# Cross attention in a three-stage decoder kernel: scores on 64 rows, probabilities split before they are turned

## The reference

```python
q = (xn @ Wq).reshape(b, n, 16, 64).transpose(0, 2, 1, 3)
kv = cn @ Wkv                      # k and v, 16 heads of 64 each
sim = jnp.einsum('bhid,bhjd->bhij', q * scale, k)
sim = jnp.where(context_mask[:, None, None, :], sim, neg)
attn = jax.nn.softmax(sim, axis=-1)
out = jnp.einsum('bhij,bhjd->bhid', attn, v)
return out.transpose(0, 2, 1, 3).reshape(b, n, INNER) @ Wo
```

## Time and profile before

| | us |
|---|---|
| median of 3 runs (lowest to highest) | 2422.98 (2419.88 to 2423.97) |
| the profiled execution | 2422.5 |
| its span, first to last instruction | 2420.4 |
| PE busy in the span | 2254.3 |
| DVE busy | 1734.5 |
| ACT busy | 1625.8 |
| POOL busy | 742.4 |
| mean granted TensorE clock | 0.962 |

### The profile page before, as it was taken

One profiled execution on the slowest core, in us unless ns is written; L12 is line 12 of the kernel. 1 busy time (PEld: TensorE's weight loads), 2 busy tenths in 40 slices (PEclk: granted clock), 3 DMA queues, 4 the chain that ended last, 5 costly groups with the idle time before them and its releaser, 6 DMA issues. The chain is left out here.

```text
span 2420.4 us, 61603 instructions
## 1 busy us (share of the span) xinstructions
PE 2254.3 (93%) x20194; PEld 1699.5 (70%) x20194; DVE 1734.5 (72%) x4722; ACT 1625.8 (67%) x3584; POOL 742.4 (31%) x1304
## 2 busy tenths in 40 slices
PE   5999999999994899999999999999999999779998
PEld 4776776786783567677767677777777777668886
DVE  4545544554643689888988898889888988466657
ACT  5546445545632688888888888888888888445444
POOL 1211211211213244444444444444444444100003
PEclk8999999999997799999999999999999999759999
DMA  5000000000002000000000000000000000203302
GB/s 140 29 1 1 0 0 0 0 0 0 0 1 74 25 15 10 14 8 14 9 13 11 12 14 8 14 8 14 8 14 8 14 1 1 71 2 105 105 1 61
DMA packets 45652, 50.08 MB, mean 21 GB/s; under 512 B 19120, under 2 KB 37664, under 8 KB 45504
## 3 DMA queue, kind: packets, MB, share of 16 engines
q1 hardware_dynamic: 45504, 48.45, 6.8%
HBM read 44.78 MB, written 3.67 MB: 20 GB/s over the span
## 5 line engine op out<-in xcount | busy, mean ns | idle before, releaser
L1398 POOL TENSOR_SCALAR p_norm<-p,p_rec 112x375 f32<-112x375 f32 x512 | 303.8, 593 | 699.7 <-DVE p_rec L1240 692.4
L1122 ACT ACTIVATE p<-s_neg,neg_max 112x375 f32<-112x375 f32 x512 | 310.6, 607 | 139.9 <-DVE neg_max L1235 107.7
L1244 DVE TENSOR_TENSOR pt_lo<-b_t,pt_hi 125x336 f16<-125x336 f32 x512 | 259.1, 506 | 96.4 <-ACT pt_hi L1128 82.4
L1013 PE MATMUL b_t<-ident,p_norm 112*125 112x112 f32 x1536 | 281.8, 293 | 15.0 <-POOL p_norm L1398 14.7
L1220 DVE SCALAR_TENSOR_TENSOR k<-b_pb,k 64x375 f16<-64x375 f32 x512 | 280.9, 549 | 13.5 <-ACT k L1113 3.2
L1235 DVE CUSTOM_DVE_ANT_0 s_neg<-b_s,mask_bias 112x375 f32<-112x375 f32 x512 | 275.7, 539 | 0.8 <-PE b_s L1007 0.7
L1113 ACT ACTIVATE k<-b_pb 64x375 f16<-64x375 f32 x512 | 243.0, 475 | 24.4 <-PE b_pb L64 21.4
L1013 PEld LDWEIGHTS b_t<-ident,p_norm 112*125 112x125 f32 x1536 | 211.2, 189 | 62.1 <-POOL p_norm L1398 39.9
L1128 ACT ACTIVATE pt_hi<-b_t 125x336 f16<-125x336 f32 x512 | 225.5, 440 | 12.0 <-PE b_t L1013 6.5
L646 POOL TENSOR_SCALAR_AFFINE_SELECT sm<-sm 112x448 f32<-112x448 f32 x128 | 71.4, 581 | 433.3 <-ACT sm L430 433.3
L1006 PE MATMUL b_s<-k,q_hi 128*112 128x375 f16 x512 | 170.1, 332 | 19.3 <-DVE neg_max L1235 18.0
(11 more groups left out here) (245 smaller groups left out, 6593.7 us busy)
## 6 DMA issues: line engine op xcount, KB each, us to landing
w_raw<-in_L_ffn_W_dram SPq DMA_DIRECT2D x16, 1024.0 KB, 7.5
ctx<-in_ctx_dram SPq DMA_DIRECT2D x32, 375.0 KB
out_dram<-c_z SPq DMA_DIRECT2D x8, 448.0 KB, 3.2
x_sb<-in_x_dram SPq DMA_DIRECT2D x1, 3136.0 KB, 19.1
ff<-in_L_attn_w_dram SPq DMA_DIRECT2D x2, 1024.0 KB, 7.3
b_stage<-in_L_xattn_Wkv_dram SPq DMA_DIRECT2D x2, 1024.0 KB, 10.5
mask<-in_mask_BxS_bf_dram SPq DMA_DIRECT2D x32, 41.0 KB, 2.6
a_raw<-in_L_attn_wq_dram SPq DMA_DIRECT2D x1, 1024.0 KB, 5.0
```

What stands on the lines that cost most here:

```text
L1013: mm = pe.transpose(t_ps[h % 2][0:JP, t * T:(t + 1) * T], p_norm[:, h % 4, t * JP:(t + 1) * JP], ident[0:T, 0:T])
L1122: act.activation(p32[:, h % 4, :], s_neg[:, h % 2, :], ACT.Exp, bias=neg_max[:, h % 4:h % 4 + 1], scale=-1.0, accum_out=p_sum[:, h % 4:h % ...
L1244: dve.tensor_tensor(pt_lo[:, h % 4, :], t_ps[h % 2][0:JP, 0:JT * T], pt_hi[:, h % 4, :], ALU.subtract).then_inc(pt_lo_done, 1)
L1398: pool.tensor_scalar(p_norm[:, h % 4, :], p32[:, h % 4, :], p_rec[:, h % 4:h % 4 + 1], 0.0, ALU.mult, ALU.add).then_inc(p_norm_done, 1)
```

## The change

Five things are done at once, all in `layer2`.

1. Keys and queries are stored as high and low tiles for pairs of heads (`k2_hi`, `k2_lo`, `q2_hi`, `q2_lo`: `KI` = 8 pairs, a head in each 64-row half). ScalarE and VectorE write a key piece with one instruction of 128 rows each instead of two of 64, a query piece with one instead of four and two. The zeros of `qz_lo` go.
2. `scores` computes two heads at once, on even steps only: three products, each as two matmuls of 64 rows, the even head on the upper and the odd one on the lower rows, into the two banks `s_ps`. It waits until all earlier heads are masked, where it waited for all but one.
3. The normalised probabilities are written as fp16 (`p_hi`, GpSimd), and VectorE computes the low half `p_lo` from `p32`, the reciprocal and `p_hi` before they are turned. TensorE turns both with six fp16 transposes against an fp16 identity, into one bank seen as 1024 fp16 columns. ScalarE takes all 672 columns out with one copy (`take_turned`); the subtraction behind the turning goes.
4. VectorE's order in a step becomes: low half of the piece, `p_low` of head s + 1, reciprocal of head s + 2, `mask_max` of head s + 4.
5. TensorE's 32 batches are all written out; the other engines keep their loops.

```diff
-k2 = sb("k2", [P, 2, H, SP2], F16)
+k2_hi, k2_lo = (sb(f"k2_{n}", [P, 2, KI, SP2], F16) for n in ("hi", "lo"))
-q2_hi = sb("q2_hi", [P, 2, H, T], F16)
-qz_lo = sb("qz_lo", [P, 2, H, T], F16)
+q2_hi, q2_lo = (sb(f"q2_{n}", [P, 2, KI, T], F16) for n in ("hi", "lo"))
-p_norm = sb("p_norm", [T, 4, S2], F32)
-pt_hi, pt_lo = (sb(f"pt_{n}", [JP, 4, JT * T], F16) for n in ("hi", "lo"))
+p_hi, p_lo = (sb(f"p_{n}", [T, 4, SP2], F16) for n in ("hi", "lo"))
+pt = sb("pt", [JP, 4, 2, JT * T], F16)
+ident16 = sb("ident16", [P, P], F16)
-t_ps = [psum(f"b_t{i}", [P, 512]) for i in range(2)]
+t_ps = [psum(f"b_t{i}", [P, 1024], F16) for i in range(2)]
...
 def scores(b, par, h):
     written(b, ("q", h // 8), ("k", h // 2))
-    at_least(pe, s_masked, H * b + h - 1)
-    ps, keys = s_ps[h % 2][0:T, 0:S2], k2[:, par, h, 0:S2]
-    pe.matmul(ps, q2_hi[:, par, h, :], keys, start=True, stop=False)
-    pe.matmul(ps, qz_lo[:, par, h, :], keys, start=False, stop=True).then_inc(s_ready, 1)
+    at_least(pe, s_masked, H * b + h)
+    for n, (q2, k2) in enumerate(((q2_hi, k2_hi), (q2_lo, k2_hi), (q2_hi, k2_lo))):
+        for r in range(2):
+            rows = slice(DH * r, DH * (r + 1))
+            mm = pe.matmul(s_ps[r][0:T, 0:S2], q2[rows, par, h // 2, :], k2[rows, par, h // 2, 0:S2],
+                           start=(n == 0), stop=(n == 2))
+            if n == 2:
+                mm.then_inc(s_ready, 1)
 def turn_scores(b, h):
-    pe.wait_ge(p_norm_done, H * b + h + 1)
-    at_least(pe, pt_lo_done, H * b + h - 1)
-    for t in range(JT):
-        mm = pe.transpose(t_ps[h % 2][0:JP, t * T:(t + 1) * T], p_norm[:, h % 4, t * JP:(t + 1) * JP], ident[0:T, 0:T])
+    pe.wait_ge(p_lo_done, H * b + h + 1)
+    at_least(pe, pt_done, H * b + h - 1)
+    for n, part in enumerate((p_hi, p_lo)):
+        for t in range(JT):
+            c = (n * JT + t) * T
+            mm = pe.transpose(t_ps[h % 2][0:JP, c:c + T], part[:, h % 4, t * JP:(t + 1) * JP], ident16[0:T, 0:T])
     mm.then_inc(t_ready, 1)
+    pe.wait_ge(pt_done, H * b + h + 2)
...
-        for n, (v2, pt) in enumerate(((v2_hi, pt_hi), (v2_hi, pt_lo), (v2_lo, pt_hi))):
+        for n, (v2, part) in enumerate(((v2_hi, 0), (v2_hi, 1), (v2_lo, 0))):
...
-                               pt[:, (h + r) % 4, keys], start=(t == 0 and n == 0), stop=last)
+                               pt[:, (h + r) % 4, part, keys], start=(t == 0 and n == 0), stop=last)
...
         if not is_last(b):
             piece(b + 1, 1 - par, s)
-        if s + AHEAD < H:
+        if s % 2 == 0 and s + AHEAD < H:
             scores(b, par, s + AHEAD)
-        elif not is_last(b):
+        elif s % 2 == 0 and not is_last(b):
             scores(b + 1, 1 - par, s + AHEAD - H)
...
+pe.wait_ge(ident16_done, 1)
...
-for h in range(AHEAD):
+for h in range(0, AHEAD, 2):
     scores(0, 0, h)
-batches(pe, body)
+for b in range(B):
+    body(b, b % 2)
...
     if kind == "q":
-        for r in range(2):
-            for rows in half_rows:
-                ins = act.activation(q2_hi[rows, par, 8 * j + r:8 * j + 8:2, :],
-                                     ps[half_rows[r], 0:4 * T].rearrange("p (m t) -> p m t", t=T), ACT.Identity,
-                                     scale=UNSCALE * DH ** -0.5)
+        ins = act.activation(q2_hi[:, par, 4 * j:4 * j + 4, :], ps[:, 0:4 * T].rearrange("p (m t) -> p m t", t=T),
+                             ACT.Identity, scale=UNSCALE * DH ** -0.5)
     elif kind == "k":
-        for r, rows in enumerate(half_rows):
-            ins = act.activation(k2[rows, par, 2 * j + r, 0:S2], ps[rows, 0:S2], ACT.Identity, scale=UNSCALE)
+        ins = act.activation(k2_hi[:, par, j, 0:S2], ps[:, 0:S2], ACT.Identity, scale=UNSCALE)
...
+    at_least(act, p_lo_done, H * b + h - 3)
...
-def turned_high(b, h):
+def take_turned(b, h):
     act.wait_ge(t_ready, H * b + h + 1)
     at_least(act, av_done, H * b + h - 3)
-    act.activation(pt_hi[:, h % 4, :], t_ps[h % 2][0:JP, 0:JT * T], ACT.Identity).then_inc(pt_hi_done, 1)
+    act.activation(pt[:, h % 4, :, :], t_ps[h % 2][0:JP, 0:2 * JT * T].rearrange("p (n c) -> p n c", n=2),
+                   ACT.Identity).then_inc(pt_done, 1)
...
     if kind == "q":
-        for r, rows in enumerate(half_rows):
-            heads = slice(8 * j + r, 8 * j + 8, 2)
-            ins = dve.scalar_tensor_tensor(qz_lo[rows, par, heads, :], ps[rows, 0:4 * T].rearrange("p (m t) -> p m t", t=T),
-                                           UNSCALE * DH ** -0.5, q2_hi[rows, par, heads, :], ALU.mult, ALU.subtract)
+        ins = dve.scalar_tensor_tensor(q2_lo[:, par, 4 * j:4 * j + 4, :], ps[:, 0:4 * T].rearrange("p (m t) -> p m t", t=T),
+                                       UNSCALE * DH ** -0.5, q2_hi[:, par, 4 * j:4 * j + 4, :], ALU.mult, ALU.subtract)
     elif kind == "k":
-        for r, rows in enumerate(half_rows):
-            h = 2 * j + r
-            ins = dve.scalar_tensor_tensor(k2[half_rows[1 - r], par, h, 0:S2], ps[rows, 0:S2], UNSCALE,
-                                           k2[rows, par, h, 0:S2], ALU.mult, ALU.subtract)
+        ins = dve.scalar_tensor_tensor(k2_lo[:, par, j, 0:S2], ps[:, 0:S2], UNSCALE, k2_hi[:, par, j, 0:S2],
+                                       ALU.mult, ALU.subtract)
...
-def turned_low(b, h):
-    dve.wait_ge(pt_hi_done, H * b + h + 1)
-    dve.tensor_tensor(pt_lo[:, h % 4, :], t_ps[h % 2][0:JP, 0:JT * T], pt_hi[:, h % 4, :],
-                      ALU.subtract).then_inc(pt_lo_done, 1)
+def p_low(b, h):
+    dve.wait_ge(p_hi_done, H * b + h + 1)
+    dve.scalar_tensor_tensor(p_lo[:, h % 4, 0:S2], p32[:, h % 4, :], p_rec[:, h % 4:h % 4 + 1], p_hi[:, h % 4, 0:S2],
+                             ALU.mult, ALU.subtract).then_inc(p_lo_done, 1)
...
-        turned_low(b, s)
-        if s + 3 < H:
-            mask_max(b, par, s + 3)
+        if s + 1 < H:
+            p_low(b, s + 1)
         elif not is_last(b):
-            mask_max(b + 1, 1 - par, s + 3 - H)
+            p_low(b + 1, 0)
         if s + 2 < H:
             sum_reciprocal(b, s + 2)
         elif not is_last(b):
             sum_reciprocal(b + 1, s + 2 - H)
+        if s + AHEAD < H:
+            mask_max(b, par, s + AHEAD)
+        elif not is_last(b):
+            mask_max(b + 1, 1 - par, s + AHEAD - H)
...
-dve.wait_ge(zeroed, 1)
 for s in range(NCH):
     piece_low(0, 0, s)
-for h in range(3):
+for h in range(AHEAD):
     mask_max(0, 0, h)
 for h in range(2):
     sum_reciprocal(0, h)
+p_low(0, 0)
...
 def normalise(b, h):
     settle(pool, passed, (p_sum_rec, H * b + h + 1), (t_ready, H * b + h - 3))
-    pool.tensor_scalar(p_norm[:, h % 4, :], p32[:, h % 4, :], p_rec[:, h % 4:h % 4 + 1], 0.0, ALU.mult,
-                       ALU.add).then_inc(p_norm_done, 1)
+    pool.tensor_scalar(p_hi[:, h % 4, 0:S2], p32[:, h % 4, :], p_rec[:, h % 4:h % 4 + 1], 0.0, ALU.mult,
+                       ALU.add).then_inc(p_hi_done, 1)
...
-pool.memset(qz_lo[:, :, :, :], 0.0).then_inc(zeroed, 1)
+pool.tensor_copy(ident16[:, :], ident[:, :]).then_inc(ident16_done, 1)
```

More of the change, by code:

```diff
@@ L823, in layer2 @@
         NCH = len(PIECES)
-        half_rows = (slice(0, DH), slice(DH, P))
         AHEAD = 4
@@ L896, in layer2 @@
         mask_m1, mask_done = sem("b_mask_m1"), sem("b_mask_done")
-        zeroed, stats_zeroed = sem("b_zeroed"), sem("b_stats_zeroed")
+        stats_zeroed = sem("b_stats_zeroed")
         pb_ready = sem("b_pb_ready")
@@ L905, in layer2 @@
         cn_hi_done, cn_done = sem("b_cn_hi_done"), sem("b_cn_done")
[L906 to L909, removed]
+        s_ready, s_masked, p_exp, p_sum_rec, p_hi_done, p_lo_done = (
+            sem(f"b_{n}") for n in ("s_ready", "s_masked", "p_exp", "p_sum_rec", "p_hi_done", "p_lo_done"))
+        t_ready, pt_done, av_done, o_hi_done, o_lo_done = (
+            sem(f"b_{n}") for n in ("t_ready", "pt_done", "av_done", "o_hi_done", "o_lo_done"))
+        ident16_done = sem("b_ident16_done")
         z_stats_done, z_mom_done, z_eps, z_rstd_done, x_done = (
@@ L1019, in values @@
                     written(b, *(("v", j) for j in range(2 * JT)))
-                pe.wait_ge(pt_lo_done, H * b + h + 2)
+                pe.wait_ge(pt_done, H * b + h + 2)
                 if h % 8 == 0:
@@ L1120, in softmax_exp @@
                 act.wait_ge(s_masked, H * b + h + 1)
-                at_least(act, p_norm_done, H * b + h - 3)
+                at_least(act, p_lo_done, H * b + h - 3)
                 act.activation(p32[:, h % 4, :], s_neg[:, h % 2, :], ACT.Exp, bias=neg_max[:, h % 4:h % 4 + 1], scale=-1.0,
                                accum_out=p_sum[:, h % 4:h % 4 + 1]).then_inc(p_exp, 1)
-            def turned_high(b, h):
+            def take_turned(b, h):
                 act.wait_ge(t_ready, H * b + h + 1)
                 at_least(act, av_done, H * b + h - 3)
-                act.activation(pt_hi[:, h % 4, :], t_ps[h % 2][0:JP, 0:JT * T], ACT.Identity).then_inc(pt_hi_done, 1)
```

(4 more changed lines are left out.)

## The result

The changed kernel takes 2456.48 us (median of 4 runs, 2455.76 to 2463.46); the kernel before took 2423.07 beside it. The ratio is 1.0147, interval [1.0126, 1.0167]: 33 us slower, where I forecast 63 us faster. The profiled run took 2463.46 us, span 2461.4, 41 us over the span before.

What follows compares the result with a forecast made beforehand. PE was taken to bound the kernel, DVE and ACT about 10% behind. Terms -1.28 + 0.3 + 0.3 - 1.1 gave -1.8 us per batch, -55 over 31; with -5 and -3, -63: 2360 us, range 2320 to 2440.

Steps and rivals of the forecast that it cites:

- Scores in row halves: Scores on PE: two 64-row halves run side by side, 0.48 instead of 0.64 us a pair, -1.28 us per batch.
- Rival 2: Scores on PE: the row halves run one after the other, +119 us, 2479; chance 0.05 with other slow slips.
- Changes of form: PE around the scores: one more array form entry per pair, +0.72, shorter load behind the values, -0.4; together +0.3 us per batch.
- Transposes: Probabilities on PE: 96 fp16 transposes at 56 ns replace 48 f32 at 107 ns, about +0.3 us per batch.
- Rival 1: Six transposes on PE: the fp16 weight load gets no shorter, 107 ns each, +152 us, 2510; chance 0.11.
- ACT: ACT's evictions: turned probabilities' copy grows to 0.73 us, key and query evictions shrink; net -2.4 of 34.1 us per batch.
- DVE: DVE's work: `p_low` costs 0.5 us (bounds 0.4 and 0.6), other pieces shrink; net -5.7 of 35.2 us per batch.
- TensorE written out: PE's loop: writing out all batches neither wins nor loses, 0 (bounds -0.2 and +0.5 us).
- Waits that are added: Scores pair waiting for masks, `p_low` for POOL: scores stay covered while DVE runs under 80% or so of PE's time.
- waits that shrink: PE's waits on other engines: 1.4 us per batch falls to 0.3, -1.1 us (bounds -2.0 and 0).
- The rival that named this place, 3: PE's waits, through POOL and ACT: stay at 1.4 us or grow by 0.5; 2395 to 2410, still faster; chance 0.18.
- The last batch: Final batch, a chain without pieces: a step falls from 2.07 to 1.7 us, -5 us.

Runs made afterwards that it cites:

- e8_half: The changed kernel with `p_lo` computed over 187 of its 375 columns, zeros turned for the rest; 2427.13 us, ratio 0.9998.
- c1_before_out: The kernel before with TensorE's 28 looped batches written out, nothing else; 2426.91 us, ratio 1.0019.
- e6_nodep: The changed kernel with TensorE turning `p_hi` twice and waiting for it alone; `p_lo` still computed but unused; 2396.39 us, ratio 0.9887.
- e9_rec: The changed kernel with VectorE's residual, statistics and preparation ahead of the mask, `p_lo` and the reciprocal ahead of the low piece; 2397.48 us, ratio 0.9893.
- a_scores: The kernel before with only the scores by row halves (paired keys and queries), TensorE still in its two-batch loop; median 2434.12 us, too scattered for a ratio.
- a1_rolled: The changed kernel with TensorE put back into its loop of two batches; 2506.46 us, ratio 1.0337.
- c2_loop4: The kernel before with four batches per turn of TensorE's loop instead of two, seven turns instead of 14; 2439.19 us, ratio 1.0043.

## Why the prediction was wrong

- *Scores in row halves*: right. The pair starts at 1505.44 and the values at 1506.06: 0.62 us, where I had 0.57, for six matmuls that would need 0.96 one after the other. Rival 2 is out.
- *Changes of form*: right. From 1505.13 to 1505.44 is 0.31 us, of which the 512-column matmul takes 0.22: 0.09 for the new entry.
- *Transposes*: right. Six in 0.34 us, 57 ns each, the weight load 137 ns. Rival 1 is out, and so is 104 ns by the Trainium skill ("TensorE: Matmul & The Clock Gate", section "LDWEIGHTS (loading the stationary operand)") for fp16 here.
- *ACT*: right. `pt` takes 727 ns (forecast 0.73).
- *DVE*: `p_lo` mis-sized. Its median is 604 ns, its mean 653, where I took 0.5 with a bound of 0.6. Its two lengths, 604 ns for 375 columns and 407 for 187 (`e8_half`), give 1.05 ns a column and 0.21 us to start; I had put the start at 0.1. 16 x 0.15 is 2.4 us of DVE a batch, which would leave 3.3 of the relief of 5.7; by the stretches view it was 3.9 (35.2 to 31.3). By `e8_half`, where 0.2 us less gave 36 us, the 0.1 us above my value is worth some 19, if in proportion.
- *TensorE written out*: wrong in its argument. I compared the loop of before with the batches written out beside it, and that is right for the body of before (`c1_before_out` 1.0019), so the 0 in the sum stands. But I hadn't seen what writing out is for: the changed body no longer turns free, and left in the loop the change would have cost another 46 us. That the 0 held is due to the body of before, not to my argument on the new one.
- *Waits that are added*: **the step that failed.** "This stays covered while DVE runs under 80% or so of PE's time" and the -1.1 us for waits that shrink. DVE was busy 769 us of 1000 (82% of PE's busy time) and idle 231, yet late. I had looked at what stands behind PE's wait, and only at utilisation on DVE's. Two dependences decide there. Before, TensorE's transposes waited for POOL, and DVE's part (a reciprocal) came early in the chain; after, DVE's `p_lo` stands between POOL and TensorE. And DVE's mask waits for a pair issued once in two steps, at the end of the even one, with up to four instructions behind it ahead of `p_lo`. PE's idle time was to shrink by 1.1 us a batch and grew by 1.8. `e6_nodep`, which takes away the dependence alone, and `e9_rec`, which changes DVE's order alone, each give back 62 or 63 us. Of my signs of being wrong one came: DVE waits for `p_hi`, 39.2 us in the 1000.

The sum with that one term replaced: 39.55 - 1.28 + 0.3 + 0.3 + 1.8 = 40.67 us a batch, measured 40.71. As a batch is PE's busy time and its idle time, this says that the busy part came out as summed (-0.68, measured -0.65). The rival that named this place, 3, had "waits grow by 0.5" at most, since it looked to POOL and ACT as the late ones. The last batch came out as taken: from the scores of its head 4 to those of head 14 it was 23.5 us before (2058.35 to 2081.82) and is 18.6 after (2107.91 to 2126.47), 4.9 less for my 5; that is 1.86 a head, where I had 1.7, and 2.35 before, where I had read 2.07 off two heads. Open are the 6 us by which the first eviction comes later (I had -3), and how the 30 us that remain in `e6_nodep` divide between POOL and DVE.

## What to carry to other kernels

A wait on an engine that works in order is priced by what is queued behind it, on its own engine as well as on the one that it waits for: list the order of a round, and ask how long after the late releaser the one instruction comes that the bounding engine needs. An engine that is 77% busy can be late six times a batch. Where a change has two halves, time each by itself: here one gained 57 us, and the other added 93 to it. And where TensorE's code stands in a loop, look for idle time without a releaser once per turn whenever the body grows, and for a lower granted clock behind it.

## What the runs showed of the hardware

- TensorE's loop in this kernel has no stop with 776 matmuls in the body, and one of 2.6 to 3.9 us per turn with 808, 872, 904 and 1552.
- Behind a stop the granted clock can fall to 0.50 for some 3 us: behind all 12 stops of `a_scores`, 4 of 12 in `a1_rolled`, 3 of 6 in `c2_loop4`.
- Transposes in fp16 stream every 57 ns with a stationary operand of 125 columns, f32 ones every 107: two fp16 halves cost 114 ns for one f32 of 107.
- ACT reads 672 fp16 columns from PSUM in 727 ns, on the line of the f32 ones (0.85 ns a column): here fp16 in PSUM is read no faster.
- Two 64-row halves run side by side: six 375-column matmuls and the change of form behind them take 0.62 us, where one after the other they would need 0.96.
